# Moving the normalisation statistics and spreading the reads of the experts' weight addresses

## The reference

```python
xn = layernorm(x)
# attention, 8 heads of 32
q, k = elu(xn @ Wq.T + bq), elu(xn @ Wk.T + bk)
u, v = silu(xn @ Wu.T + bu), silu(xn @ Wv.T + bv)
energy = (q @ k.T) * causal_mask           # no softmax
out = rms_norm(energy @ v, scale)
attention = (u * out) @ Wo.T + bo
# experts: each token goes to one of 8
top1 = argmax(xn @ Wg.T)
xhat = normalise(xn)                       # a second time
y[token] = gelu((xhat * s_e + b_e) @ W1_e + b1_e) @ W2_e + b2_e   # e = top1[token]
```

## Time and profile before

| quantity | value |
|---|---|
| time, median of 3 runs | 342.39 us (341.08 to 342.73) |
| the profiled execution's own time | 343.99 us |
| span of that execution (first to last instruction) | 342.2 us |
| busy: PE / DVE / POOL / ACT | 272.4 / 206.7 / 186.5 / 158.7 us |
| mean granted clock of TensorE | 0.908 of full speed |
| load of one input tile, issue to landing | 4.1 us |
| one indirect DMA of `scatter`, issue to landing | 2.5 us |

### The profile page before, as it was taken

How to read it: one execution, slowest core, us unless ns; L and a number is a source line. 1 busy time by engine, 2 the same in 40 slices (tenths; PEclk the granted TensorE clock), 3 DMA queues, 4 the chain that set the end, 5 groups by cost and what they waited for, 6 DMA issues and landing times. The chain is left out here.

```text
span 342.2 us, 7905 instructions
## 1 busy us (share of the span) xinstructions
PE 272.4 (80%) x2912; PEld 231.8 (68%) x2912; DVE 206.7 (60%) x530; ACT 158.7 (46%) x296; POOL 186.5 (54%) x414
## 2 busy tenths in 40 slices
PE   2598997999799799799979955995776999697600
PEld 2487785888679588687868945884756878576400
DVE  6787492695488179369648914781486355555621
ACT  2358256545834845664492536351221656444200
POOL 6336666575577567547657641762474002756671
PEclk9999899899899989989989995999698899989955
DMA  7997013004003201300402100110004466889985
GB/s 262 316 345 219 3 63 124 2 33 156 0 2 112 77 2 62 124 3 18 162 9 64 63 1 2 61 63 2 1 17 131 130 187 212 267 231 344 302 286 173
DMA packets 33510, 39.61 MB, mean 116 GB/s; under 512 B 2481, under 2 KB 30657, under 8 KB 33473
## 3 DMA queue, kind: packets, MB, share of 16 engines
q1 hardware_dynamic: 30176, 30.69, 27.6%
q0 software_dynamic: 3072, 8.39, 7.8%
q10 hardware_dynamic: 224, 0.03, 0.1%
HBM read 20.23 MB, written 18.87 MB: 114 GB/s over the span
## 5 line engine op out<-in xcount | busy, mean ns | idle before, releaser
L1161 POOL DMA_INDIRECT x_in<-ys,rows x32 | 32.6, 1018 | 41.5 <-DMA ys<-y_blk 32.0
L581 ACT ACTIVATE e_neg<-ring,cols 128x512 f32<-128x512 f32 x32 | 22.0, 689 | 50.1 <-PE ring L245 50.1
L243 PE MATMUL ring<-xn_hi,w_hi 128*128 128x512 f32 x96 | 41.1, 429 | 1.8 <-DVE xn_lo L727 1.7
L742 DVE TENSOR_TENSOR energy<-ring,causal 128x512 f32<-128x512 f32 x64 | 39.5, 682 | 0.1
L245 PE MATMUL ring<-xn_hi,w_lo 128*128 128x512 f32 x96 | 39.3, 409 | 0.0
L244 PE MATMUL ring<-xn_lo,w_hi 128*128 128x512 f32 x96 | 39.2, 409 | 0.0
L1150 POOL DMA_INDIRECT xs<-x_in,rows x32 | 32.8, 1026 | 11.6 <-issue 7.3
L766 DVE TENSOR_TENSOR g<-ring,uT 128x512 f32<-128x512 f32 x16 | 11.0, 687 | 37.3 <-ACT sq L598 20.3
L365 PE MATMUL ring<-xT_blk,w_blk 128*128 128x128 f32 x156 | 26.3, 294 | 4.5 <-DVE w_blk L855 4.1
L286 PE MATMUL kv_bank<-v_tok,k_tok 128*32 128x32 f32 x480 | 9.0, 228 | 26.0 <-ACT k_tok L594 25.3
L757 DVE TENSOR_TENSOR state<-state,kv_bank 128x256 f32<-128x256 f32 x30 | 12.6, 421 | 26.4 <-PE kv_bank L286 25.0
(11 more groups left out here) (158 smaller groups left out, 759.7 us busy)
## 6 DMA issues: line engine op xcount, KB each, us to landing
xs<-blank SPq DMA_DIRECT2D x4, 1280.0 KB, 10.9
x_blk<-xs SPq DMA_DIRECT2D x20, 256.0 KB, 3.4
ys<-y_blk SPq DMA_DIRECT2D x20, 256.0 KB, 3.2
x_in<-in_x SPq DMA_DIRECT2D x8, 512.0 KB, 4.1
o<-in_x SPq DMA_DIRECT2D x8, 512.0 KB, 4.8
out<-o SPq DMA_DIRECT2D x8, 512.0 KB, 4.5
energy<-in_w_in SPq DMA_DIRECT2D x4, 256.0 KB, 4.5
energy<-in_w SPq DMA_DIRECT2D x1, 512.0 KB, 6.7
```

Of the source, the lines that this page charges most:

```text
L243: pe.matmul(bk, w_h(k), x_h(k), start=(first and k == 0), stop=False, skip_group_check=skip)
L581: act.activation(e_neg[t][:, :], bk[:, :], ACT.Exp, bias=vecs[:, col:col + 1]).then_inc(s[f"{w}_exp"], 1)
L742: dve.tensor_tensor(energy[:, t, m, :].rearrange("p (c n) -> p c n", c=CH), bank(f"s{t}{m}", n)[:, :].rearrange("p (c x) -> p c x", c=CH), ...
L1161: pool.indirect_dma_start(out=x_in[n % 3][:, c, :], out_offset=None, in_=ys[0:blocks * P, :], in_offset=bass.IndirectOffsetOnAxis(ap=rows[ ...
```

## The change

On DVE `norm_stats(m)` goes from behind `gated(i, 0)` to the head of the tick. On POOL `norm_scalars` of a tile goes ahead of the scatter of the tile two before it, that is into the tick before. `expert_of_blocks` becomes `find_experts(n)`, which is run in each of the 8 ticks and works out tile `i` alone (the final sum is over all tiles so far); the factor `WROW` goes into the constant `which`. Each of the ticks 0 to 6 reads four addresses: two after `find_experts`, ahead of `gated(i, 1)`, and two between `xnT_lo` and `reciprocal`. Tick 7 reads one, and the other ten are read in every second block, from block 0 to block 18.

```diff
@@ find_experts and load_expert @@
-            def expert_of_blocks(tiles):
...
+            def find_experts(n):
+
+                dve.wait_ge(s["booked"], booked(n, "first"))
                 dve.wait_ge(s["row_const"], 1)
...
+                begun = past[:, n, :]
+                dve.tensor_scalar(begun, first_block[:, n, :], block_col[:, :], None, ALU.is_le).then_inc(s["past"], 1)
...
+                dve.tensor_tensor(begun, begun, which[:, :], ALU.mult).then_inc(s["expert1"], 1)
+                dve.wait_ge(s["expert1"], n + 1)
+                dve.tensor_reduce(expert_f[:, :], flat(past[:, 0:n + 1, :]), AX.X, ALU.add).then_inc(s["expert2"], 1)
+                dve.wait_ge(s["expert2"], n + 1)
+                dve.tensor_copy(expert[:, :], expert_f[:, :]).then_inc(s["expert"], 1)
+
+            def load_expert(k, n):
+
+                dve.wait_ge(s["expert"], n + 1)
+                weights_at[k] = dve.value_load(expert[k:k + 1, 0:1], min_val=0, max_val=(NE - 1) * WROW)
@@ DVE, tick @@
                 norm_next = m < TILES
+                if norm_next:
+                    norm_stats(m)
                 elu(n, "k", 0, bank("k0", i))
...
                 gated(i, 0, bank("att0", i))
-                if norm_next:
-                    norm_stats(m)
                 for c in range(CH):
                     logits_out(n, c, bank(f"v{c}", i))
                 choose_expert(n)
-                if i == TILES - 3:
-
-                    expert_of_blocks(TILES - 2)
-                if i >= TILES - 3:
-                    j = (i - (TILES - 3)) * EARLY // 2
-                    load_experts(j, j + EARLY // 2)
+
+                find_experts(i)
+                load_expert(CH * i, i)
+                load_expert(CH * i + 1, i)
                 gated(i, 1, bank("att1", i))
...
                     xnT_lo(m, 1, bank("xnT1", i))
+                load_expert(CH * i + 2, i)
+                load_expert(CH * i + 3, i)
                 reciprocal(i)
@@ DVE, last tick @@
-                expert_of_blocks(TILES)
+                find_experts(i)
                 mean_square(i, bank("ssq", i))
-                load_experts(EARLY, EARLY + 4)
+                load_expert(CH * i, i)
@@ DVE, expert blocks @@
-                    if EARLY + 4 + k < BLOCKS:
-                        load_experts(EARLY + 4 + k, EARLY + 5 + k)
+
+                    if k % 2 == 0 and CH * (TILES - 1) + 1 + k // 2 < BLOCKS:
+                        load_expert(CH * (TILES - 1) + 1 + k // 2, TILES - 1)
@@ POOL @@
             book(0)
+            norm_scalars(2)
             scatter(0)
...
                 n, m = i + 1, i + 2
-                if m < TILES:
-                    norm_scalars(m)
                 squares(i)
...
                 book(n)
+                if m + 1 < TILES:
+                    norm_scalars(m + 1)
                 scatter(n)
```

More of the change, by code:

```diff
@@ L31 @@
 PAIRS = (BLOCKS + 1) // 2
-EARLY = CH * (TILES - 2)
 BACK = CH + NE - 1 + 9
@@ L148, in build @@
         counts = sb("counts", [P, (CH + 1) * NE])
-        which = sb("which", [P, TILES, NE])
+        which = sb("which", [P, NE])
         fill = sb("fill", [P, NE])
@@ L822, in dve_program @@
             weights_at = {}
-            def expert_of_blocks(tiles):
-                time = 1 if tiles < TILES else 2
-                dve.wait_ge(s["booked"], booked(tiles - 1, "first"))
+            def find_experts(n):
+                dve.wait_ge(s["booked"], booked(n, "first"))
                 dve.wait_ge(s["row_const"], 1)
[L830 to L834, removed]
-                                         ).then_inc(s["expert0"], 1)
[L836 to L847, removed]
+                begun = past[:, n, :]
+                dve.tensor_scalar(begun, first_block[:, n, :], block_col[:, :], None, ALU.is_le).then_inc(s["past"], 1)
+                dve.wait_ge(s["past"], n + 1)
@@ new lines, in find_experts @@
+                dve.scalar_tensor_tensor(begun, end_block[:, n + 1, :], block_col[:, :], begun, ALU.is_gt, ALU.mult
+                                         ).then_inc(s["expert0"], 1)
+                dve.wait_ge(s["expert0"], n + 1)
+                dve.tensor_tensor(begun, begun, which[:, :], ALU.mult).then_inc(s["expert1"], 1)
+                dve.wait_ge(s["expert1"], n + 1)
+                dve.tensor_reduce(expert_f[:, :], flat(past[:, 0:n + 1, :]), AX.X, ALU.add).then_inc(s["expert2"], 1)
@@ L1188, in pool_program @@
             for e in range(NE):
-                pool.memset(which[:, :, e:e + 1], float(e))
+                pool.memset(which[:, e:e + 1], float(e * WROW))
             pool.memset(fill[:, :], float(P))
```

## The result

The changed kernel takes 316.67 us, median of 4 runs (313.75 to 317.01); the kernel before, run beside it, 341.74 (339.8 to 342.73). The ratio is 0.925, 95% interval 0.918 to 0.933. Forecast were 327.4 with a range of 320.0 to 333.5: the direction is right, the gain is 25 instead of 15. The profiled execution of after takes 316.96 with a span of 314.7, that of before 343.99 with 342.2.

What follows compares the result with a forecast made beforehand. PE's waits at `kv_pair`, through ACT's late `shift` and DVE's twelve reads in ticks 5 and 6, were taken as the bound. 343.99 - 19.8 + 4.0 (clock) + 0.8 (blocks) = 329.0; from the median 342.39 - 15.0 = 327.4, range 320.0 to 333.5.

Steps and rivals of the forecast that it cites:

- the 1.25 per tick for the reads ahead of `reciprocal`: DVE at the start of a tick: two address reads lengthen the way to the next elu by 1.25.
- the 0.8 per tick for the clock: PE around the second scores: half-speed stretches after new stops, 0.8 per tick within 0 to 1.6, 4.0 in five ticks.
- The 2.27 wait for `shift` goes: ACT ahead of `norm_apply`: `shift` from POOL comes at about K + 15.5, so the 2.27 wait disappears.
- my path: DVE from K, the start of `kv_pair(n, 0)` on PE, through the third mask: 14.16, then the second scores can start.
- `find_experts` and the first pair of reads lie in 4.06 of idle time: DVE ahead of `gated(i, 1)`: the 2.4 of `find_experts` and two reads fits into 4.06 of idle time.
- The expected stops of 0.7 and 1.3: PE waits some 2.0 for DVE in two pieces, for k's elu before q1 and for masks before the second scores.
- Rival 2: Ticks and blocks: no slow stretch and the blocks lose nothing, 322.6; chance 0.25.
- Rival 1: Ticks: each has the slow stretch, 8.0 instead of 4.0, so 331.4; chance 0.28.
- The blocks lose 0.8: Expert blocks 12 to 18: four more visible reads of 0.49 each; bounds 0 and 1.9, 0.8 taken.
- the three reads fewer in tick 7 are worth nothing: Tick 7: three reads fewer gain nothing, as PE waits there for `x_blk`, whose chain goes through POOL.
- rival 3: Ring of `x_in`: load, statistics, scalars and scatter wait on each other; 8.2 to spare, price 0, else 345; chance 0.03.
- rival 4: POOL late with `shift`, over 6 later than forecast, ticks 0 to 4 unchanged: 331.6, or 333 with uncovered reads; chance 0.07.

Runs made afterwards that it cites:

- experiment 3: Changed kernel with POOL's scalars put back behind `book_next`, statistics staying at the head of the tick: 322.51 us, ratio 0.941.
- experiment 2: Changed kernel without the two reads ahead of `reciprocal`: 316.45 us, ratio 0.923; with all four reads of a tick there: 319.18, 0.938.
- experiment 4: Changed kernel with four more `bn_stats` at the head of ticks 0 to 5: 323.2 us, ratio 0.947; with eight, on the slow chip: 346.23, 0.960.
- experiment 1: Kernel before with only the address reads spread: 329.04 us, ratio 0.961; with only statistics and scalars moved: 330.54, ratio 0.965.
- experiment 5: Changed kernel with `find_experts` and first reads behind `gated(i, 1)`, block reads moved: 328.42 us; only first reads behind: 314.78, beside the unaltered changed kernel at 317.72.

## Why the prediction was wrong

The mechanism was right, the sum was not: 15.0 were forecast, and the span shrank by 27.5 (342.2 less 314.7; the medians by 25.1, since the traced execution of before lay above its median). The terms that failed are the 1.25 per tick for the reads ahead of `reciprocal`, which measured 0.0, and the 0.8 per tick for the clock, which measured 0. By the steps of the sum:

1. **The 2.27 wait for `shift` goes.** Right; experiment 3 shows that without POOL's new order it does not.
2. **Two reads ahead of `reciprocal` cost 1.25 per tick.** This is the step of the loop that failed. They cost 0.0 (experiment 2). I had measured reads in the earlier trace rows, where DVE had nothing left to execute and each of twelve showed in full. Here the queue goes on reading while `xn_lo` executes, and `rms` comes as late anyway. The forecast's own block rows showed this (every second read is hidden there), but it was not carried over to the tick. Without that term my path is 14.16 - 1.25 = 12.91 to the end of the third mask, and 12.95 was measured; the other DVE rows were right to 0.2, and errors of 0.3 (the wait for `rms`) and -0.2 (`add_attention`) cancel. In five ticks this is 5.4 (27.7 less 26.65 each). Tick 6 was 25.45 instead of 26.0, K of tick 0 0.4 earlier than forecast, K to `ms` 0.1 shorter: 1.1 more.
3. **`find_experts` and the first pair of reads lie in 4.06 of idle time and cost nothing in ticks 1 to 4.** Not quite. With the wait for `shift` gone the idle time there is 1.7 (1.74 in the kernel with the statistics alone), less than the 2.4 that goes in: the 0.5 ahead of K. The forecast used cover that its own first step removes. In its loop this was counted, as the chain ran through DVE.
4. **The clock, 0.8 per tick, 4.0 in all.** It cost 0: 1.00 in ticks 1 to 6. There were two reasons. The expected stops of 0.7 and 1.3 shrank to a wait of 0.7 inside the second scores, since step 2 was wrong; and neither stops of the expected size (0.44 and 1.3) nor longer ones (1.74 and 1.3) bring the clock down at that place (experiment 4). The price of a slow stretch, 1.6 on the loop, was also too high: it measured 1.1 in experiment 1, and 0 in experiment 3, where the statistics stand at the head. Rival 2 had the clock right, but not the loop. Rival 1, and with it the reading of the Trainium skill (Perfetto Trace Analysis, Matmul Optimizations) by which the broken-up start of the tick costs a slow stretch each time, does not hold for stops of this size at this place (1.74 ahead of matmuls of 512 columns, 1.3 inside the scores). Why 2.2 ahead of `kv_pair` do it in some ticks and not in others (experiment 1) stays open (nor why one of the stops of 1.71 in experiment 3 did it); what part the narrow matmuls around it have was not tried.
5. **The blocks lose 0.8.** From `ms` to the end it was 1.2 less. The blocks do take 2.7 per pair as forecast, up to block 18, and blocks 10 to 18 together take 1.3 more than before, against the 1.9 forecast. But block 0 starts 2.5 earlier behind `ms` (22.13 against 24.63). PE waits for `x_blk` ahead of it both times (1.94 before, 2.76 after); behind that wait the granted clock of 4 us was 0.60 before and is 1.00 after. This I can't put down to the change: the changed kernel on the chip of experiment 5 has 0.70 there and block 0 at 24.34. In all executions traced off the slow chip that have the tick 7 and the blocks of the changed kernel, `ms` to the end takes 94.8 to 99.0. So the 2.0 between forecast and result lie within what the same code varies by, and that the three reads fewer in tick 7 are worth nothing stands uncontradicted. What decides the clock at the first `x_blk` stays open.
6. **The ring of `x_in` has 8.2 to spare (rival 3), the scalars come in time (rival 4).** Both right: no wait of `norm_stats` for its load in the ticks, none of ACT for `shift`.

Together: 6.5 in the loop, 4.0 of clock, 2.0 in the blocks, which is the 12.5 by which the forecast of the span was off (the median was off by 10.7). With the reads and the clock at 0 alone, the forecast would have been 327.4 - 6.25 - 4.0 = 317.2 (the same 1.25 in tick 6 is worth 0.2, as PE's own 12.2 bounds it then). That this meets 316.67 is in part luck, as it leaves out the 0.9 by which five ticks of 26.65 are longer than the forecast's rows without the reads (12.91 + 13.56 = 26.47 each), and the 2.0 of the blocks. Both ends of the range had the reads as a certain term of 1.25; only the clock and the blocks were given bounds. The upper end, 333.5, does not come out of its terms either: rival 1 with the whole 1.9 is 332.5, and rival 4 is 332.7.

## What to carry to other kernels

Price a register read by what its engine still has to execute when the queue reaches it: behind 1.3 us of vector work two reads were free and two more cost their full 0.6 each. When a wait is taken away, work out again the idle time that other edits hide in; here 4.06 became 1.7. A slow stretch of one engine costs time only where the others wait for that engine: 1.1 in one order of the same tick, 0 in another. And before small vector operations are moved into a gap, look at what GpSimd runs in that gap.

## What the runs showed of the hardware

- The queue of an engine reads registers while the engine executes: two reads beside 1.28 of `xn_lo`, 0.0 more; four, 1.25 more.
- TensorE's clock fell behind stops of 2.2 to 2.4 ahead of 32-column matmuls in three of six ticks (experiment 1), behind one of five stops of 1.25 to 1.71 at that place (experiment 3), and in none of the ten ticks of experiment 4 behind stops of 0.44 or 1.74 ahead of 512-column matmuls and 1.3 inside the scores.
- A slow stretch cost a tick 1.1 in experiment 1 and 0 in experiment 3. At the start of the blocks the same kernel had 1.00 in one execution and 0.70 in another, and its first block 2.2 later in the second.
- Vector operations on 128x8, 0.17 to 0.23 by themselves, take 0.7 to 1.2 beside GpSimd's operations on 128x512, and end with them.
- The kernel before took 340.2 to 342.5 on three chips and 361.87 on a fourth.
